# Moving the first layer normalisation of batches 4 to 15 from VectorE to ScalarE in an attention and mixture-of-experts kernel

## What is computed

```python
x = x + _L0_xattn_ref(_layernorm(x), ctx, mask, Wq, Wk, Wv, Wo)   # 16 heads of 8, masked keys, softmax
x = x + _L0_ffn_ref(_layernorm(x), gate_w, wi_gate, wi_up, wo)    # 8 experts, top 2, silu(gate) * up
# _layernorm: (x - mean) / sqrt(var + 1e-5), per row of 128
```

## Time and profile before

| | us |
|---|---|
| median of 3 runs (385.52 to 385.85) | 385.84 |
| the profiled execution, its own time | 385.02 |
| its span in the trace | 383.2 |
| PE busy | 348.0 (91% of the span) |
| DVE busy | 251.2 (66%) |
| POOL busy | 228.4 (60%) |
| ACT busy | 193.4 (50%) |

### The profile page before, as it was taken

One profiled execution on the slowest core, in us unless ns is written; L12 is line 12 of the kernel. 1 busy time (PEld: TensorE's weight loads), 2 busy tenths in 40 slices (PEclk: granted clock), 3 DMA queues, 4 the chain that ended last, 5 costly groups with the idle time before them and its releaser, 6 DMA issues.

```text
span 383.2 us, 8985 instructions
## 1 busy us (share of the span) xinstructions
PE 348.0 (91%) x3013; PEld 304.9 (80%) x3013; DVE 251.2 (66%) x933; ACT 193.4 (50%) x439; POOL 228.4 (60%) x195
## 2 busy tenths in 40 slices
PE   5899799999999996668999999999999999999970
PEld 2566577687778764558999999999999999999970
DVE  5898999999999996604455554645546455465440
ACT  3578677787888873303344444434434343344320
POOL 6373512667667777740464573864848638368673
PEclk9899999999999998598999999999999999999995
DMA  6899301222323222124137245463373544724232
GB/s 179 244 359 297 92 7 23 63 67 67 82 55 118 72 66 68 53 60 124 15 30 168 33 42 162 37 150 54 37 173 34 114 82 38 176 21 38 28 34 21
DMA packets 41159, 34.33 MB, mean 90 GB/s; under 512 B 8337, under 2 KB 37521, under 8 KB 40977
## 3 DMA queue, kind: packets, MB, share of 16 engines
q1 hardware_dynamic: 26592, 23.67, 21.0%
q0 software_dynamic: 13568, 9.58, 18.2%
q10 hardware_dynamic: 960, 0.60, 0.6%
HBM read 21.12 MB, written 17.73 MB: 101 GB/s over the span
## 4 chain that ended last, share of the span: by engine, by line
PE 68%; DVE 14%; POOL 6%; issue 4%; ACT 3%; DMA 3%; SPq 1%; POOLq 1%; DVEq 0%; ACTq 0%
PE bank L921 18%; PE bank L676 11%; PE bank L678 10%; PE bank L677 10%; PE bank L779 5%; POOL slots L441 4%; DVE mneg L1027 4%; PE bank L747 3%; PE bank L770 2%; PE bank L912 2%; DVE rall L1077 1%; PE bank L797 1%; DMA maskr<-in_mask 1%; PE bank L730 1%; PE bank L731 1%
## 5 line engine op out<-in xcount | busy, mean ns | idle before, releaser
L475 POOL DMA_INDIRECT out<-ys,idx x80 | 125.0, 1562 | 83.8 <-DVE ys L1308 52.1
L1335 DVE TENSOR_TENSOR h<-sg,bank 128x256 f32<-128x256 f32 x160 | 66.2, 419 | 86.8 <-ACT sg L661 78.7
L661 ACT ACTIVATE sg<-bank 128x256 f32<-128x256 f32 x160 | 61.5, 385 | 107.7 <-PE bank L678 107.2
L676 PE MATMUL bank<-ex_hi,w_hi 128*128 128x256 f32 x320 | 95.8, 299 | 1.0 <-DVE ex_lo L1289 0.3
L678 PE MATMUL bank<-ex_lo,w_hi 128*128 128x256 f32 x320 | 89.5, 280 | 0.0
L677 PE MATMUL bank<-ex_hi,w_lo 128*128 128x256 f32 x320 | 89.5, 280 | 0.0
L921 PE MATMUL bank<-w_raw,h 128*128 128x128 f32 x640 | 78.0, 275 | 0.8 <-DVE h L1335 0.8
L921 PEld LDWEIGHTS bank<-w_raw,h 128*128 128x128 f32 x640 | 74.9, 192 | 0.9 <-DVE h L1335 0.9
L441 POOL DMA_INDIRECT slots<-rall,slot x64 | 62.7, 980 | 18.4 <-issue 17.5
L676 PEld LDWEIGHTS bank<-ex_hi,w_hi 128*128 128x128 f32 x320 | 60.9, 190 | 4.1 <-issue 2.5
L677 PEld LDWEIGHTS bank<-ex_hi,w_lo 128*128 128x128 f32 x320 | 61.0, 190 | 0.0
(11 more groups left out here) (122 smaller groups left out, 536.7 us busy)
## 6 DMA issues: line engine op xcount, KB each, us to landing
slots<-in_empty SPq DMA_DIRECT2D x8, 660.0 KB, 10.7
xl<-slots SPq DMA_DIRECT2D x7, 660.0 KB, 7.3
w_raw<-in_wgu SPq DMA_DIRECT2D x8, 512.0 KB, 3.7
w_raw<-in_wdn SPq DMA_DIRECT2D x8, 256.0 KB, 4.3
out<-X SPq DMA_DIRECT2D x16, 128.0 KB
X<-in_x SPq DMA_DIRECT2D x3, 512.0 KB, 5.5
out<-ys,idx POOLq DMA_INDIRECT x80, 3.3
slots<-rall,slot POOLq DMA_INDIRECT x64
```

Source lines behind the costliest of these rows:

```text
L475: nc.gpsimd.indirect_dma_start(out=out[:, :], out_offset=bass.IndirectOffsetOnAxis(ap=IDX[v][:, j:j + 1], axis=0), in_=YS[c][:, t, :], in_ ...
L661: nc.scalar.activation(SG[m % 2][:], GATE_PS[m % 2][:, 0:2 * P], ACT.Silu).then_inc(sg_ready, 1)
L676: nc.tensor.matmul(ps, hi, m_hi, start=True, stop=False)
L1335: nc.vector.tensor_tensor(H[n % 2][:, f, :], SG[m % 2][:], UP_PS[m % 2][:, 0:2 * P], ALU.mult).then_inc(h_ready, 1)
```

## The change

`norm(b)` for b = 4 to 15 leaves DVE and becomes two ACT instructions at the very end of ACT's step i = b-3, behind `stack_queries(i+1, 1)`. Where DVE computed (x - mean) * rstd with two per-row operands, ACT computes rstd * x + shift, also with two per-row operands. DVE prepares shift = -mean * rstd for four tiles in one instruction, in every odd step from 1 to 11. `norm(0)` to `norm(3)` stay on DVE.

```diff
+SHIFTED = [b for b in range(4, 16) if b % 2 == 0]
...
+        SHIFT = s1("shift", [P, TILES])
...
+            def norm(b):
+
+                act.wait_ge(shift_ready, b // 2 - 1)
+                act.wait_ge(tx_full, b - 1)
+                for t in range(2):
+                    tile = 2 * b + t
+                    ins = nc.scalar.activation(XN[b % 2][:, t, :], X[:, tile, :], ACT.Identity, bias=SHIFT[:, tile:tile + 1], scale=RSTD[:, tile:tile + 1])
+                ins.then_inc(xn_ready, 1)
...
                 if there(i + 1):
                     stack_queries(i + 1, 1)
+                if i >= 1 and there(i + 3):
+                    norm(i + 3)
...
+            def shift(b):
+
+                k = b // 2
+                tiles = slice(4 * k, 4 * k + 4)
+                dve.wait_ge(rstd_ready, k + 1)
+                nc.vector.scalar_tensor_tensor(out=SHIFT[:, tiles], in0=MV[:, tiles, 0], scalar=-1.0, in1=RSTD[:, tiles],
+                                               op0=ALU.mult, op1=ALU.mult).then_inc(shift_ready, 1)
...
-                if there(i + 3):
-                    norm(i + 3)
+                if i == 0:
+                    norm(3)
+                if i + 3 in SHIFTED:
+                    shift(i + 3)
```

More of the change, by code:

```diff
@@ L225, in program @@
         ve_ready, rstd_ready = sem("ve_ready"), sem("rstd_ready")
+        shift_ready = sem("shift_ready")
         xn_ready, tx_full, xt_ready = sem("xn_ready"), sem("tx_full"), sem("xt_ready")
```

## The result

The changed kernel takes 389.12 us (median of 4 runs, 388.88 to 389.24) against 385.68 (385.44 to 385.85) of the kernel before in the same session: a ratio of 1.0083, 95% interval 1.0064 to 1.0102, so slower by 3.4 us (by the interval, 2.5 to 3.9). The profiled execution took 389.02, 4.0 more than that of before. It was forecast at 389.8, with a range of 385.5 to 391.0.

The account below looks back on a forecast made before the run. PE bounds steps 5, 7 and 9 to 13; held time 3.7 us plus 0.5 for slower queries less 0.2 from DVE gives +4.0 on 385.02, plus 0.8 to the median: 389.8 us, range 385.5 to 391.0.

Parts of the forecast that it names:

- The reading by steps: Steps 5, 7 and 9 to 13 are PE-bound; in steps 4, 6 and 8, after moments, PE waits for DVE's maximum.
- DVE gives 0.2 us: Without xn, err of step 5 moves up to its guess, shortening step 6's wait; gain in all 0.2 us.
- The formula of the held time: PE held before queries by N + 0.90 less the distance from last qs copy to queries; 3.7 us over seven steps.
- N: Time the moved pair occupies on ACT, taken as 0.8 us, between 0.41 and 0.90.
- the slower queries: In the seven PE-bound steps, queries after a wait for xt take 0.70 instead of 0.63 us; 0.5 us in all.
- The sign that PE would be idle: PE idle before queries, released by ACT's xt, 0.5 to 0.65 us in steps 5, 7 and 9 to 13.
- The covers in steps 4, 6 and 8: PE's wait for DVE, 0.56 us at least or up to 0.9, hides a hold of about 0.65; nothing counted.
- The case of broken covers: Rival: with N at 0.90 or more, steps 4, 6 and 8 grow by up to 0.2 us each; 391.0 us, chance 0.05.
- Nothing back behind step 13: POOL's inverse deviation in step 14 waits for DVE, so POOL, its last transfers and part two all move later.
- the forecast's own range: The forecast mechanism's total, 387.1 us (N = 0.41 with the slower queries) to 390.7 (N = 0.90).
- DVE's relief as 2 us: Rival: DVE bounds, four xn on the chain at 0.5 us go, less the shifts; 384.0 us, chance 0.13.
- the pair almost for nothing: Rival: with N = 0.41 held time is 1.0 us, less 0.2; 386.6 us, no difference, chance 0.11.

Follow-up runs that it names:

- e6_dve_relief: Changed kernel without the ACT pair and the shift, nothing in their place (normalisation of batches 4 to 15 left out): 385.02 us against 385.19 of the kernel before.
- e5_act_added: Kernel before with the ACT pair added at the same place, result unread, DVE keeping its normalisations: 389.64 us against 385.19 of the kernel before.
- e9_spread_dve: e7_spread with every normalisation kept on DVE: 423.73 us against 429.21 of the kernel before, ratio 0.9832, in a disturbed session.
- e8_split_again: Same kernel as e1_split, run again for a full time: 385.07 us against 385.19 of the kernel before, ratio 0.9998.
- e7_spread: e1_split with moments of batches 6 to 15 moved to where DVE's normalisation stood, two tiles a step: 381.59 us against 385.19 of the kernel before.
- e1_split: Changed kernel with the ACT pair split around the copy of the queries' first half, mid next step: 427.68 us against 425.46 of the kernel before, disturbed.

## Why the prediction was right

- **What bounds.** The reading by steps held: in the PE-bound steps PE's wait for xt is the new wait, and the steps with moments before them did not change (8.18 stays 8.18 in steps 4 and 8). DVE is a little more loaded than the 6.94 to 7.16 named: 7.23 and 7.26 in steps 11 and 12.
- **DVE gives 0.2 us.** The size holds for the relief alone: `e6_dve_relief` gains 0.21 in step 6 and nothing in steps 4 and 8. In the changed kernel, though, the 0.20 by which step 6 shrank (8.39 to 8.19) is not DVE's doing: `e5_act_added` has the same 8.18 with all of DVE's work, since the longer step 5 lets DVE catch up. The sum counted the gain once, so it came out; its reason was not the one given. That `err` starts with its guess is not all that limits the relief either: in `e9_spread_dve` `err` came 0.78 us after its guess and the step was 0.14 longer, so in a step without moments at its end the relief might bring little even without the wait for the guess. That was not tried by itself.
- **The formula of the held time.** Predicted with N = 0.8 for steps 5, 7, 9, 10, 11, 12 and 13: 0.49, 0.49, 0.50, 0.65, 0.48, 0.55 and 0.53, and 0.07 each for the slower queries, 4.2 together. Measured, after less before: 0.47, 0.54, 0.53, 0.67, 0.54, 0.59 and 0.59, 3.9 together; N accounts for 0.14 of the difference. Step 5 is less than its share because before it held 0.06 that disappears in every variant: it takes 7.21 in the runs without held time, and `e5_act_added`, without DVE's relief, has the 7.73 of the changed kernel. The sign that PE would be idle for 0.5 to 0.65 us ahead of the queries did not come: the profile lists 0.29 to 0.44. The queries start later by what was forecast (0.47 us in step 7, from 0.94 to 1.41 behind the step's start), but the instruction in front of them is shown at its full 0.40 us, where a queued one would have followed 0.23 behind its start, so the idle time listed is shorter than the delay. Step 10 took 8.03, a little over the 7.7 to 7.9.
- **N.** Taken as 0.8 between 0.41 and 0.90, measured 0.78. (Guess is not quite the only ACTIVATE of the loop from SBUF to SBUF in fp32, `expd` with 128x4 in 0.20 us is another; nothing hangs on it.) The lower bound was exact for a pair without such operands (0.41), and the choice of the upper end was right for the reason given, the per-row operands, which cost 0.09 us each. The Trainium skill's figures for them ("ScalarE: Activation LUTs", "What ACT_TABLE_LOAD costs": about 93 ns for a pointer operand) agree with what the traces show for a pair, 0.19 us for the first operand and 0.18 for the second.
- **The covers in steps 4, 6 and 8.** PE was held there too, with 0.44 us of idle time listed in each, and the steps grew by nothing. The case of broken covers did not occur, but it was nearer than the forecast had it. It had put the held time at 0.65 (0.72 with the slower queries) and the cover at 0.56 or 0.9; by the smaller reading the cover would have broken at N = 0.8 already. From start to start the cover was 0.73 in step 8, and 0.68 of it is used: some 0.05 us more of N, and these steps would have grown as well.
- **Nothing back behind step 13.** Right: 3.74 us at step 14, and POOL's inverse deviation starts at 137.51 instead of 133.75, 3.76 later; 4.0 at the end, where 3.7 and 4.0 can't be told apart.
- **The total.** 4.0 us were forecast. The steps show 3.7, the two profiled executions differ by 4.0, and the medians by 3.4. That the profiled executions meet the 4.0 is luck: the profiled execution of the changed kernel took about its median and that of before 0.7 us less than its own, and 0.3 lies in the part that the change doesn't touch. The time of 389.8 was 0.7 too high for the same reason: it added the 0.8 us between the profiled execution and the median of before. The upper end of the forecast's own range, 390.7, left out the 0.2 of DVE; with it, 390.5.
- **The rivals.** DVE's relief as 2 us is refuted by `e6_dve_relief`; the pair almost for nothing is what happens at another place (`e8_split_again`), not at this one; the changed kernel's trace has two table loads, as that of before.

## What to carry to other kernels

Work that is moved to a less busy engine costs what its place in that engine's order costs: look at what is queued behind it and who waits for that, and put it where the engine waits for others, split if a gap is too small. Before a step is taken off an engine, look at what the instruction behind it waits for; if that starts with its other operand, the time saved turns into idle time. It can be filled with work of the same engine that stands at a worse place, as in `e7_spread`; but try that move by itself first, since in `e9_spread_dve` it brought 2.21 of the 2.65 us of four steps with nothing taken off the engine.

## What the runs showed of the hardware

- A per-row operand costs an ACT instruction 0.09 us, for the scale and for the shift alike, and it lengthens the time until the next instruction can start, not only its own: 128x128 pairs occupy 0.41, 0.60 and 0.78 us with none, one and two.
- The ACT copy behind such a pair takes 0.35 us (once 0.36) instead of 0.37.
- A matmul that starts at once when its operand arrives takes longer than one that was queued: the two parts of the queries take 0.70 instead of 0.62 or 0.63 us in all eleven steps of the changed kernel in which PE waited for xt, and the next instruction starts 0.34 or 0.35 us behind their start; the queued ones of steps 4 to 13 before have it 0.26 to 0.29 behind.
- The idle time that the profile lists ahead of a matmul is less than the time that was lost: PE's wait in step 8 before is listed as 0.56 us and is 0.73 from start to start; the 0.29 listed in step 7 after go with queries that start 0.47 later.
- On two of the chips used all kernels took some 40 us more, that of before too, and those with a trace went from steps of 7 to 8 us to steps of mostly 9 to 14 us from about 68 us on. Every one of these traces names a releaser "remote" there that the traces of undisturbed runs don't show; in `e1_split`:

```profile
ACT xt L531 <- remote: 5.9, 2, 3.3
...
DVE mneg L1052 <- remote: 3.9, 4, 1.4
```

What it is was not found out; that queues stalled, as one of the expectations has it, is not shown either.
